# Attention block with a routed expert layer: stationary weight columns in gate and up, a half-precision down product for all late tiles, and two arrays of sums

## The reference

```python
def _L0_attn_ref(x, w_attn, b_attn, w_proj, b_proj):     # x: (4, 512, 256), 16 heads of 16
    qkv = x @ w_attn + b_attn                            # q and k are then rotated
    attn = softmax(causal scores) * E ** (-0.5)
    return (attn @ v).reshape(B, T, E) @ w_proj + b_proj

def _L0_ffn_ref(hidden_states, router_w, ws, w2s):       # 2048 tokens, 8 experts, top 2, FFN 512
    probs = jax.nn.softmax(x @ router_w.T, axis=-1)
    top_w, top_i = jax.lax.top_k(probs, TOP_K)
    top_w = top_w / jnp.sum(top_w, axis=-1, keepdims=True)
    combine = zeros.at[arange(T)[:, None], top_i].add(top_w)
    for e in range(E):
        gate = x @ ws[e, :I, :].T
        up = x @ ws[e, I:, :].T
        h = jax.nn.silu(gate) * up
        out = out + combine[:, e:e + 1] * (h @ w2s[e].T)

x = _layernorm(x + _L0_attn_ref(x, ...))
x = _layernorm(x + _L0_ffn_ref(x, ...))
```

## Time and profile before

| | us |
|---|---|
| median of 3 runs | 513.27 (512.68 to 515.3) |
| the profiled execution | 515.15 |
| its span, first to last instruction | 513.3 |
| mean granted clock of PE | 0.947 of full |

### The profile page before, as it was taken

One profiled execution on the slowest core, in us unless ns is written; L12 is line 12 of the kernel. 1 busy time (PEld: TensorE's weight loads), 2 busy tenths in 40 slices (PEclk: granted clock), 3 DMA queues, 4 the chain that ended last, 5 costly groups with the idle time before them and its releaser, 6 DMA issues.

```text
span 513.3 us, 9836 instructions
## 1 busy us (share of the span) xinstructions
PE 433.3 (84%) x3058; PEld 264.0 (51%) x3058; DVE 334.8 (65%) x1184; ACT 313.9 (61%) x460; POOL 244.5 (48%) x332
## 2 busy tenths in 40 slices
PE   1999898999796999889973899999999999999700
PEld 0555444445453555445532567666666666666500
DVE  7156987876779887977698424577657666762234
ACT  0486549997866677665997167555535666653115
POOL 0063411123565487555825375644555665554322
PEclk9999969999999999979996799999999999999955
DMA  8368899822246214412321024333343333343254
GB/s 274 69 166 246 258 353 330 255 77 63 63 123 213 93 52 141 122 41 85 124 83 32 10 35 91 73 66 49 53 63 53 59 57 55 62 63 43 28 167 173
DMA packets 32978, 57.25 MB, mean 112 GB/s; under 512 B 5025, under 2 KB 23585, under 8 KB 31394
## 3 DMA queue, kind: packets, MB, share of 16 engines
q1 hardware_dynamic: 18306, 39.60, 24.6%
q0 software_dynamic: 7488, 10.27, 12.9%
q10 hardware_dynamic: 7136, 6.77, 4.2%
HBM read 38.64 MB, written 17.97 MB: 110 GB/s over the span
## 4 chain that ended last, share of the span: by engine, by line
PE 44%; DVE 23%; DMA 18%; issue 8%; ACT 6%; POOLq 1%; ACTq 0%; POOL 0%; SPq 0%; DVEq 0%
DMA sum_rows<-PT,IDXA 16%; PE PS L1587 9%; DVE PS L995 8%; PE PS L298 6%; PE PS L1614 5%; PE PS L1366 4%; PE PS L1405 4%; PE PS L1440 3%; PE PS L1387 2%; PE PS L305 2%; ACT PT L779 2%; DVE W L1132 2%; PE PS L1606 2%; PE PS L1459 1%; ACT W L817 1%
## 5 line engine op out<-in xcount | busy, mean ns | idle before, releaser
L995 DVE CUSTOM_DVE_ANT_0 PS<-PS,CB 128x512 f32<-128x512 f32 (+3 forms) x256 | 121.2, 516 | 35.2 <-PE PS L1366 33.9
L1587 PE MATMUL PS<-W,PT 128*128 x468 | 114.9, 382 | 4.0 <-issue 3.9
L779 ACT ACTIVATE PT<-PS 128x1024 f32<-128x1024 f32 x80 | 81.3, 1021 | 36.8 <-PE PS L1388 36.3
L730 POOL DMA_INDIRECT sum_rows<-PT,IDXA x39 | 62.1, 1593 | 57.6 <-DMA sum_rows<-PT,IDXA 21.4
L1366 PE MATMUL PS<-KQ 96*128 96x512 bf16 (+3 forms) x256 | 64.5, 316 | 13.1 <-DVE MX L995 11.9
L1587 PEld LDWEIGHTS PS<-W,PT 128*128 128x128 f16 x468 | 43.8, 98 | 43.2 <-issue 6.5
L1387 PE MATMUL PS<-KQ 104*128 104x512 bf16 (+3 forms) x256 | 60.8, 308 | 0.4 <-ACT PT L779 0.4
L714 POOL DMA_INDIRECT KQ<-x_rows,IDXA x39 | 40.0, 1027 | 30.4 <-DVE WS L1249 18.1
L1405 PE MATMUL PS<-PT,VA 128*32 128x256 f32 (+3 forms) x512 | 45.0, 446 | 4.7 <-ACT PT L779 4.7
L1388 PE MATMUL PS<-CB 128*128 128x128 bf16 x256 | 48.1, 223 | 0.0
L1366 PEld LDWEIGHTS PS<-KQ 96*128 96x128 bf16 x256 | 20.0, 100 | 46.3 <-DVE MX L995 33.4
(11 more groups left out here) (230 smaller groups left out, 891.4 us busy)
## 6 DMA issues: line engine op xcount, KB each, us to landing
W<-w1T SPq DMA_DIRECT2D x8, 1024.0 KB, 8.5
qk_parts<-W SPq DMA_DIRECT2D x32, 192.0 KB, 3.2
KQ<-qk_parts SPq DMA_DIRECT2D x32, 192.0 KB, 2.9
KQ<-qk_parts SPq DMA_DIRECT2D x64, 64.0 KB, 3.0
x_rows<-X1S ACTq DMA_DIRECT2D x4, 516.0 KB, 3.6
W<-xT SPq DMA_DIRECT2D x4, 512.0 KB, 6.7
KQ<-qk_parts SPq DMA_DIRECT2D x16, 128.0 KB, 3.0
sum_rows<-X ACTq DMA_DIRECT2D x4, 512.0 KB, 3.2
```

Of the source, the lines that this page charges most:

```text
L730: pool.indirect_dma_start(acc_dram, bass.IndirectOffsetOnAxis(ap=IDXA[:, j, 0:1], axis=0), YS[j % TRIO], None, compute_op=ALU.add).then_in ...
L779: act.activation(PT[n][:, :], STb[slot_of(k, n)].rearrange("p a n -> p (a n)"), ACT.Exp).then_inc(s["exp"], 1)
L995: last = dve.tensor_tensor_reduce(src, src, maskS[:, TT * P - w:], 1.0, LOW, ALU.add, ALU.max, MX[p][:, h, i:i + 1])
L1587: last = mm(dst, XGT[j % TRIO][:, x_part, k, :], w1h[:, bass.ds(at, UNIT)], start=(k == x_part == w_part == 0), stop=(k == KC - 1 and x_pa ...
```

## The change

Gate and up change roles. The stationary operand is now a block of 128 x 128 weights, the moving one the 128 tokens, and the hidden values lie on the partitions of the result. A half is thus 24 matmuls of 128 columns where it was 6 of 512. Each weight block has an address of its own, so there are 16 register operations in a half where there were 4. The hidden values come out as the down product wants them: `hidden_T`, `split_hidden_T` and the copies behind them go, and with them bank 3 and bank 5.

All tiles from 17 on (`SPLIT_FROM = NEARLY`, which is 17) now have the down product in two f16 parts, one tile late. The scale is no longer one for each token row but one for each expert, a bound from the squares of its weights (`bounds`, a few small DVE operations in tile 14; `HSJ` and `WSJ` hold it for each tile). The row maxima and reciprocals go.

Even tiles are added into `sum_rows`, odd tiles into a second array `odd_rows`. A tile's addition waits for the one two tiles before it. The second array is zeroed by two transfers of 1 MB from ACT's queue in the attention part. At the end both are loaded (16 transfers of 256 KB, on SP's and ACT's queues) and added: chunks 0, 2, 4, 6 on DVE, chunks 1, 3, 5, 7 on POOL.

```diff
-SPLIT_FROM = 17
-LAST = NTILES - 5
-NSPLIT = LAST - SPLIT_FROM
-HSCALE = 2.0 ** -14
+SPLIT_FROM = NEARLY
+NSPLIT = NTILES - SPLIT_FROM
 N2 = FF // P * NX * E // 512
+HBOUND = 2.0 ** 8
...
-        SIL, HH = PT[2][:, 0:512], PT[2][:, 512:1024]
-        HT = PT[3][:, 0:512].rearrange("p (k t) -> p k t", k=4)
+        SIL = PT[2][:, 0:512]
+        HT = [PT[3][:, 512 * n:512 * n + 512] for n in range(2)]
         YS = [PT[4][:, 256 * n:256 * n + 256] for n in range(3)]
         JUNK = PT[0][:, :]
-        HHI, HLO = ([v.bitcast(F16) for v in pair] for pair in ((PT[0][:, 0:256], PT[1][:, 768:1024]), (PT[0][:, 256:512], PT[4][:, 768:1024])))
-        HTH = PT[0][:, 512:1024].bitcast(F16).rearrange("p (r k t) -> p r k t", r=2, k=FF // P)
+        HH = PT[0][:, 0:512]
+        HHI = [PT[2][:, 512 + 256 * n:768 + 256 * n].bitcast(F16) for n in range(2)]
+        HLO = [PT[n][:, 768:1024].bitcast(F16) for n in (1, 4)]
...
+        def summed(j):
+
+            return s_acc[j % 2], 16 * (j // 2 + 1)
...
             def add_result(j):
 
                 pool.wait_ge(f["ys"], j + 1)
-                if j:
-                    pool.wait_ge(s_acc, j * 16)
-                pool.indirect_dma_start(acc_dram, bass.IndirectOffsetOnAxis(ap=IDXA[:, j, 0:1], axis=0), YS[j % TRIO], None,
-                                        compute_op=ALU.add).then_inc(s_acc, 16)
+                if j >= 2:
+                    pool.wait_ge(*summed(j - 2))
+                if j == 1:
+                    pool.wait_ge(s_zero2, 2 * 16)
+                pool.indirect_dma_start((acc_dram, odd_dram)[j % 2], bass.IndirectOffsetOnAxis(ap=IDXA[:, j, 0:1], axis=0), YS[j % TRIO], None,
+                                        compute_op=ALU.add).then_inc(s_acc[j % 2], 16)
...
+            def zero_rows(n):
+
+                zeros = CB[:, 4 * P:6 * P].bitcast(F32)
+                act.dma_start(odd_dram[n * NTOK // 2:(n + 1) * NTOK // 2, :].rearrange("(p n) (h f) -> p (n h) f", p=P, h=2),
+                              zeros.unsqueeze(1).broadcast_to([P, NTT, P])).then_inc(s_zero2, 16)
...
             def hidden_high(j):
-                i = j - SPLIT_FROM
-                act.wait_ge(f["ri"], i + 1)
-                act.activation(HHI[i % 2], HH, ACT.Copy, scale=RI[:, i:i + 1]).then_inc(f["hhi"], 1)
-
-            def hidden_columns(j):
-                act.wait_ge(f["th2"], j - SPLIT_FROM + 1)
-                act.wait_ge(f["yp"], j)
-                act.activation(HTH[:, 0, :, :].rearrange("p k t -> p (k t)"), HPh[0], ACT.Copy).then_inc(f["hta"], 1)
+
+                act.wait_ge(f["h"], j + 1)
+                if j >= SPLIT_FROM + 2:
+                    act.wait_ge(f["yp"], j - 1)
+                act.activation(HHI[j % 2], HH, ACT.Copy).then_inc(f["hhi"], 1)
...
+            for j in range(SPLIT_FROM, NTILES):
                 silu(j)
                 if j + 1 < NTILES:
                     columns(j + 1)
-                if j == LAST + 1:
-                    split_result(LAST - 1)
-                result(j - 1)
-            result(NTILES - 1)
+                if j == SPLIT_FROM:
+                    result(j - 1)
+                hidden_high(j)
+                if j > SPLIT_FROM:
+                    split_result(j - 1)
+            split_result(NTILES - 1)
...
+                dve.wait_ge(f["ws"], j + 1)
+                dve.tensor_tensor(WS2[:, i:i + 1], WS[:, j:j + 1], WSJ[:, i:i + 1], ALU.mult).then_inc(f["ws2"], 1)
                 dve.wait_ge(f["sil"], j + 1)
                 dve.wait_ge(f["u"], j + 1)
-                if i == 0:
-                    dve.wait_ge(f["th"], SPLIT_FROM)
-                else:
+                if i:
                     dve.wait_ge(f["hlo"], i)
-                dve.scalar_tensor_tensor(HH, U, CW[:, :], SIL, ALU.mult, ALU.mult).then_inc(f["h"], 1)
-                dve.wait_ge(f["h"], j + 1)
-                link(dve.tensor_reduce(HM[:, i:i + 1], HH, AX.X, ALU.max, apply_absolute_value=True))
-                link(dve.tensor_scalar(HB[:, i:i + 1], HM[:, i:i + 1], 1e-30, HSCALE, ALU.max, ALU.mult))
-                dve.reciprocal(RI[:, i:i + 1], HB[:, i:i + 1]).then_inc(f["ri"], 1)
-                dve.wait_ge(f["ws"], j + 1)
-                dve.scalar_tensor_tensor(WS2[:, i:i + 1], WS[:, j:j + 1], HB[:, i:i + 1], CC[:, :], ALU.mult, ALU.mult).then_inc(f["ws2"], 1)
+                dve.scalar_tensor_tensor(HH, U, HSJ[:, i:i + 1], SIL, ALU.mult, ALU.mult).then_inc(f["h"], 1)
 
             def hidden_low(j):
 
-                i = j - SPLIT_FROM
-                dve.wait_ge(f["hhi"], i + 1)
-                dve.scalar_tensor_tensor(HLO[i % 2], HH, RI[:, i:i + 1], HHI[i % 2], ALU.mult, ALU.subtract).then_inc(f["hlo"], 1)
-
-            def hidden_columns(j):
-
-                dve.wait_ge(f["th2"], j - SPLIT_FROM + 1)
-                dve.wait_ge(f["yp"], j)
-                dve.tensor_copy(HTH[:, 1, :, :].rearrange("p k t -> p (k t)"), HPh[1]).then_inc(f["htd"], 1)
+                dve.wait_ge(f["hhi"], j - SPLIT_FROM + 1)
+                if j >= SPLIT_FROM + 2:
+                    dve.wait_ge(f["yp"], j - 1)
+                dve.tensor_tensor(HLO[j % 2], HH, HHI[j % 2], ALU.subtract).then_inc(f["hlo"], 1)
...
-                if j:
-                    dve.wait_ge(f["th"], j)
-                dve.scalar_tensor_tensor(HH, U, CW[:, :], SIL, ALU.mult, ALU.mult).then_inc(f["h"], 1)
+                if j >= 2:
+                    dve.wait_ge(f["yp"], j - 1)
+                dve.scalar_tensor_tensor(HT[j % 2], U, CW[:, :], SIL, ALU.mult, ALU.mult).then_inc(f["h"], 1)
                 if j == 0:
                     post(B - 1, 1, TB[1])
-                dve.wait_ge(f["th"], j + 1)
-                if j:
-                    dve.wait_ge(f["yp"], j)
-                dve.tensor_copy(HT.rearrange("p k t -> p (k t)"), HP).then_inc(f["ht"], 1)
...
             def half(j, e, dst, n, done):
 
-                for k in range(KC):
-                    for x_part, w_part in ((0, 0), (0, 1), (1, 0)):
-                        at = (e + k * NX) * (4 * UNIT) + (2 * n + w_part) * UNIT
-                        last = mm(dst, XGT[j % TRIO][:, x_part, k, :], w1h[:, bass.ds(at, UNIT)], start=(k == x_part == w_part == 0), stop=(k == KC - 1 and x_part == 1))
+                for c in range(FF // P):
+                    for k in range(KC):
+                        for w_part, x_parts in ((0, (0, 1)), (1, (0,))):
+                            at = (e + k * NX) * (4 * UNIT) + (2 * n + w_part) * UNIT + c * P
+                            for x_part in x_parts:
+                                last = mm(dst[:, c * P:(c + 1) * P], w1h[:, bass.ds(at, P)], XGT[j % TRIO][:, x_part, k, :],
+                                          start=(k == x_part == w_part == 0), stop=(k == KC - 1 and w_part == 1))
                 last.then_inc(done, 1)
...
-            def hidden_T(j):
+            def down(j, e):
                 pe.wait_ge(f["h"], j + 1)
-                if j:
-                    pe.wait_ge(f["ht"], j)
-                for k in range(FF // P):
-                    last = nc.tensor.transpose(HP[:, k * P:(k + 1) * P], HH[:, k * P:(k + 1) * P], ident)
-                last.then_inc(f["th"], 1)
-
-            def down(j, e):
-                pe.wait_ge(f["ht"], j + 1)
                 if j:
                     pe.wait_ge(f["ys"], j)
                 for k in range(FF // P):
-                    last = mm(YP[:, 0:E], HT[:, k, :], W2[k][:, bass.ds(e * E, E)], start=(k == 0), stop=(k == FF // P - 1))
+                    last = mm(YP[:, 0:E], HT[j % 2][:, k * P:(k + 1) * P], W2[k][:, bass.ds(e * E, E)], start=(k == 0), stop=(k == FF // P - 1))
                 last.then_inc(f["yp"], 1)
 
-            def split_hidden_T(j):
-
+            def split_down(j, e):
                 i = j - SPLIT_FROM
-                if i:
-                    pe.wait_ge(f["hta"], i)
-                    pe.wait_ge(f["htd"], i)
-                else:
-                    pe.wait_ge(f["ht"], SPLIT_FROM)
                 pe.wait_ge(f["hhi"], i + 1)
                 pe.wait_ge(f["hlo"], i + 1)
-                for r, part in enumerate((HHI[i % 2], HLO[i % 2])):
-                    for k in range(FF // P):
-                        last = nc.tensor.transpose(HPh[r][:, k * P:(k + 1) * P], part[:, k * P:(k + 1) * P], IDH[:, :])
-                last.then_inc(f["th2"], 1)
-
-            def split_down(j, e):
-                i = j - SPLIT_FROM
-                pe.wait_ge(f["hta"], i + 1)
-                pe.wait_ge(f["htd"], i + 1)
                 pe.wait_ge(f["ys"], j)
                 if i == 0:
                     pe.wait_ge(s["lo2"], N2)
                 for k in range(FF // P):
-                    for h_part, w_part in ((0, W2H), (0, W2L), (1, W2H)):
-                        last = mm(YP[:, 0:E], HTH[:, h_part, k, :], w_part[k][:, bass.ds(e * E, E)],
-                                  start=(k == 0 and h_part == 0 and w_part is W2H), stop=(k == FF // P - 1 and h_part == 1))
```

(38 more changed lines are left out.)

155 lines of the change are left out of this document (53 added, 102 removed).

## The result

The changed kernel takes 557.2 us (median of 4 runs, 554.74 to 558.22), the kernel before 513.14 beside it. The ratio is 1.084, with a 95% interval of 1.080 to 1.089. The predicted 546 was too low by 11 us, and its range of 531 to 562 held the time.

A forecast was written before the change was run, and what follows sets the result against it. Before, PE's array and the addition chain were taken as nearly equal limits; after, PE's instruction stream. Terms +0.5, +0.5, +2.5, +27.9, -3.1, +4.0 sum to +32.3 on 515.15, 547.5 us profiled, 546 us as median; range 531 to 562.

The forecast's parts named there:

- two limits of one height: Tiles 17 to 38: PE's 4.57 us and the addition chain's 4.65 us nearly equal; removing one alone would give little.
- The array: Gate and up: 48 matmuls at 0.056 us, 2.70 against 2.58 us; array work of a later tile 4.24 us.
- The sequencer: PE's instruction stream in tiles 1 to 38: 0.123 us a step, 38 or 43 steps a tile, would bind PE.
- first stretch, a tile: Tiles 1 to 16: 38 steps plus 0.8 us for reading the expert's number, 5.47, taken as 5.45 us.
- extras in the first stretch: Tiles 1 to 16: of 7.0 us of extra work and stalls, 2 us stay for instructions of the extra products.
- late tile: Tiles 17 to 38: 43 steps, 6.09 us, taken as 6.0 us; over 21 distances +27.9 us.
- The sums and the end: Last gate to the end's loads -3.1 us; the end +4.0 us, with POOL's four additions beside DVE's work.
- The small terms: Attention part +0.5 us (0 to 3) for DVE reductions and zeros; tile 0 +0.5 us for up's second half.
- PE's busy share falls in the expert layer: Sign of being right, expert layer: PE's busy share falls although nothing is waited for, idle time put down to "issue".
- the register operations hide: Rival, expert layer: a register operation costs little more than 46 ns, the array sets the pace, 496 us; chance 0.10.
- rival 1: Gate and up: array slower at 128 columns, weight blocks loading visibly between matmuls, 546 to 570 us; chance 0.05.
- The clock: Rival, expert layer: with the sequencer in front the clock falls to 1.2 GHz, 650 us; chance 0.04.

## Why the prediction was right, and where it was short

**What bounds the kernel before.** That two limits of one height held the late tiles was half right. PE's 4.57 us held them; the chain of additions cost only its lag at the end. Two arrays alone brought no tile closer.

**The array.** 48 x 0.056 us stood in the sum. With fixed addresses it is 0.056 a matmul and 4.21 us a late tile, against the 4.24 forecast. Confirmed.

**The sequencer.** The mechanism is shown from three sides: without the register operations the changed kernel gains 60 us, with as many of them in the old role it is 55 us slower than before (44 in the new one), and a third less or more array work is worth 2 us. The size was short. The step was read from a free run of 13 in 1.6 us as 0.123. The trace after has 0.124 for most, but one in eight is longer, and the mean of gate and up is 0.133. Half of the difference of 0.010 could have been read in tile 3. By the starts of its records, the first 9 of the 13 steps (gate, rows_T's wait and up) take 1.153 us, 0.128 each; the wait for down and three steps of down take 0.455 us, 0.114 each, two of them behind an ALU_OP. The mean of 0.123 thus already had the shorter steps of down in it, and the prediction put it on gate and up too. Going down from 6.09 to 6.0 us counted them once more. The other half, the long steps, is not to be seen in a run that short. The sum's terms, side by side:

| | predicted | measured |
|---|---|---|
| first stretch, a tile | 5.45 | 5.73 |
| extras in the first stretch | 2 | 93.2 - 16 x 5.73 = 1.5 |
| late tile | 6.0 | 6.25 |

For tiles 1 to 38 the forecast was +30.4 and the result +38.8, 8.4 more. The rows of the late tile above say where it lies: 37 distances x 33 steps of gate, rows_T and up x 0.010 us are +12.2, by far the most. The two tile prices had been rounded down from 5.47 and 6.09, +2.2; for the late one my reason was that steps behind ALU_OP are shorter (they are, by 12 ns), and the step of down came out at 0.125 all the same, +0.5. Against them stand one wait that I counted and that costs no step of its own (21 x 0.123 = -2.6), the reading of the expert's number (0.75 instead of 0.8, -1.9), the wait ahead of down (0.11 instead of 0.123, -0.6) and the extras (-0.5). That is +9.3; the late tiles' mean of 6.21 instead of 6.25 takes the rest. The step of 0.133 is the upper edge of the spread that the prediction gave it, which by itself stands for 561 us. The range held, but only just where its main term is concerned, and the time stayed below the edge because smaller terms went the other way.

**The sums and the end.** The part from the last gate to the loads was right to 0.3 us (-3.1 and -2.8). The end was priced at +4.0 and measured +6.5. The first pair is later by 0.8 instead of 0.6, and DVE's four additions cost 2.9 instead of 3.2. What was missing is the 2.6 us that POOL's additions, "beside DVE's work", take from DVE's small operation. An operation moved to another engine was costed at nothing with its cover named, and the cover did not hold. Nor did the prediction see that the 16 loads alone, without any addition, would lengthen the end by 3.3 us.

**The small terms.** Tile 0 took 7.9 to 8.9 us in all eleven traces, and the first gate started at 281.2 to 285.1 us. The +0.5 for each can be called neither right nor wrong.

**The signs in the profile.** Right were 1248 register operations 124 ns apart, additions that no longer wait for each other, and matmuls 87 ns apart where about 84 was said. "PE's busy share falls in the expert layer" was half wrong: it fell from 98.89 of 99 us to 124.15 of 130.37 (95%) in the late tiles, but rose from 84.00 of 86 to 93.02 of 93.20 in the first stretch, and over the span it went from 84 to 85%. Only 9.1 us of idle time before gate and up are put down to "issue". By busy time PE looks as well used as before, although the kernel with fixed addresses does the same matmuls 60 us sooner.

**The rivals.** That the register operations hide (496 us) described the kernel with fixed addresses, which took 497.5; it does not describe this one, where a step costs 0.133 and not under 0.10. The sign of rival 1, matmuls over 80 ns apart, was also met by the forecast's own 84; only fixed addresses told the two apart. The clock did not fall: 1.00 in both stretches.

No version that computes the whole result beats the kernel before. Fixed addresses are no solution, since a tile's expert is known only at run time. Code for each expert behind a branch, with constant addresses, could gain up to the 16 us between 514 and 497.5. It was not tried, and what the branches cost is open.

## What to carry to other kernels

Count an engine's register operations, not only its matmuls: with run-time addresses each cost the sequencer 0.13 us here. By an estimate from that and from 0.056 us for 128 columns, an address should serve some 300 columns of matmuls or more, or the array waits for it. A stream that is bound by its sequencer looks busy; compare the distance of the matmuls with what they take in a row elsewhere. Before a chain of waits is relieved, ask whether the engine beside it would be faster without it, and before work is put on another engine "beside", look for a run in which both work at once.
